# An expert layer that starts from an early tile map: 24 tiles mapped before the attention ends, 16 shared blocks in front and 16 behind

## The chip, the core and the metric

The kernel runs on one core of a Trainium2 chip. A time is the device time of one execution in microseconds (us). Three executions of the kernel before took 761.66, 758.09 and 762.01 us, with a median of 761.66 us. The core's engines run side by side, each through its own list of instructions in order: TensorE (PE in the rows, PEld for its weight loads), VectorE (DVE), ScalarE (ACT), GpSimd (POOL) and SyncE (SP), which issues most of the DMAs. They meet at semaphores.

## What is computed

Two layers, each an attention and then a mixture of 8 experts, on 32 x 128 = 4096 tokens of width 128. Only the last two parts matter here:

```python
x = x + attention_1(layernorm(x), ctx)        # 16 heads, window of 64, rotary angles
xf = layernorm(x).reshape(4096, 128)
scores = softmax(xf @ gate_w.T)
idx = top_k(scores + gate_b, 2)               # two of 8 experts for each token
rw = scores at idx, else 0
expert(x, w1, b1, w3, b3, w2, b2) = silu((x @ w1 + b1) * (x @ w3 + b3)) @ w2 + b2
y = sum over experts of rw * expert_e(xf)     # the routed part: 8192 (token, expert) pairs
z = expert_shared(xf)                         # the shared part: every token
x = x + y + z
```

## The kernel before

**The attention of layer 1** handles one block of 128 tokens in a step k of a loop to k = 32, and the last blocks in twelve named steps, `TAIL`: "divide", "turn last but one", "products last but one", "normalise last", "turn last", "products last", "softmax last", "choose last", "rank last", "fills", "tiles" and "maps". The router runs along with it, over groups of 4 or 2 blocks (`GROUPS_AT[1]`). VectorE chooses the experts of a group (`choose`, L829 to L847), TensorE counts how many tokens each expert has so far (`ranks`, L1155; the rank of the group at step k of `RANK_AT`), VectorE adds that to the running totals `carry` and writes each token's place (`place_reads` and `place`, L850 to L870). GpSimd then scatters the tokens' rows to their expert's region in DRAM, two indirect DMAs for each block (`scatter`, L533). The first four groups (16 blocks) are ranked by k = 24 and the last one in "rank last".

**The maps.** In "fills", "tiles" and "maps" VectorE turns the final totals into two tables (L1013 to L1045): `emap`, the expert of each tile, and `rowmap`, the DRAM row where the tile starts. A tile is 128 rows of one expert, and there are `SLOTS` = 71 of them. SyncE waits for the totals, fills up each expert's last tile (`fill_up`, L351), waits for the maps and for every scatter (`rows_in_place`), and only then loads tile 0.

**The expert layer** (`gated_experts`) works in units (`UNITS`). A shared unit is two blocks of the shared expert, which needs no map: first products `widen` (L1776), two copies on ScalarE (L1666, L1667), the product of the halves on VectorE (`hidden`, L1707), silu on ScalarE (L1672, L1674), second products `narrow` (L1789), and an addition to `x` on VectorE (L1722). A routed unit is two tiles. SyncE loads them into one of 16 places of `xs` (L1591), TensorE turns them (`take`, L1756), VectorE copies the expert's weights (`w1_copies`, L1697), then the same chain (L1770, L1663, L1704, L1672, L1789), and VectorE scales each result into one of 8 places of `ys` (L1716). GpSimd scatters each tile's results to DRAM by an indirect DMA (`send`, L1640), with indices that `note` (L1632) has copied from `xs` to `xi` once for each pair. VectorE may write a place of `ys` only when the scatter of eight tiles earlier has landed.

The order is 11 shared units (22 blocks, `SHARED_FIRST`), 36 routed units, 5 shared units. Each unit has two halves in every engine's list, and a half stands behind each of the twelve `TAIL` steps (`SLOTS_AT`); the rest follow. The PE halves are: first half `widen` of its own unit, second half `narrow` of the unit two before.

**The end.** SyncE waits for all scatters (`results_stored`), loads the results of all tokens in ten DMAs (L1608), VectorE adds them in eight steps of four blocks (`add_results`, L1730 and L1731), and SyncE stores `x` in five DMAs (L1614).

## Time and profile before

| | us |
|---|---|
| median of three runs | 761.66 |
| the profiled execution | 763.85 |
| its span, first to last instruction | 762.0 |
| PE busy in the span | 667.7 (88%) |
| DVE busy | 545.3 (72%) |
| POOL busy | 500.1 (66%) |
| ACT busy | 410.8 (54%) |
| mean granted TensorE clock | 0.954 of full |

In the profile, all times are from the span's start. The attention of layer 1 lies at 400 to 594 us, its twelve last steps with shared units between them at 594 to 620, more shared units to 634, the routed units to 722, five shared units to 736, and the loading, adding and storing of the end to 762. A timeline row is: start, duration, engine, line, operation, output<-input, shapes, count, and in brackets how long the engine sat idle before it and what released it.

### The profile page before, as it was taken

To read this page: it belongs to the slowest core of one execution; us is meant where nothing else is said; L and a number is where in the kernel's file an instruction comes from. 1 tells how busy PE (TensorE), PEld (TensorE's weight loads), DVE (VectorE), ACT (ScalarE), POOL (GpSimd) and SP (SyncE) were. 2 spreads that over 40 slices of the span, in tenths; PEclk is the share of its full clock that TensorE was granted. 3 is DMA by queue.
4 is the path that set the end of the run, shared out by engine and by line. 5 is a ranking of instruction groups with operands and counts; after the bars stand their busy time and mean duration, and the time that the engine had idled before them with its cause. 6 is when DMAs were issued, how large, how long until landed. Compare 5 with 4: busy or idle time off the path is not lost.

```text
span 762.0 us, 20655 instructions
## 1 busy us (share of the span) xinstructions
PE 667.7 (88%) x6884; PEld 560.4 (74%) x6884; DVE 545.3 (72%) x1634; ACT 410.8 (54%) x1054; POOL 500.1 (66%) x850
## 2 busy tenths in 40 slices
PE   6599999988798999799998999999998779999950
PEld 4477777766567989799985777777776569999950
DVE  3579999999842674244425889999998667888735
ACT  2246555555554333234415777777775657777740
POOL 5354488788764897578745553777877762888850
PEclk9799999999999999899997999999999999999985
DMA  8192000000104522322211100111001133333229
GB/s 233 45 375 52 5 27 26 27 30 31 36 33 108 158 58 75 110 72 68 72 57 53 29 17 28 44 41 54 24 27 33 36 105 83 104 103 104 76 80 288
DMA packets 60988, 57.69 MB, mean 76 GB/s; under 512 B 11347, under 2 KB 54006, under 8 KB 60342
## 3 DMA queue, kind: packets, MB, share of 16 engines
q1 hardware_dynamic: 52246, 38.41, 18.0%
q0 software_dynamic: 8640, 17.97, 6.9%
q8 instruction: 58, 0.95, 0.5%
q14 instruction: 44, 0.36, 0.2%
HBM read 33.77 MB, written 22.08 MB: 73 GB/s over the span
## 4 chain that ended last, share of the span: by engine, by line
POOL 26%; PE 26%; DVE 22%; issue 16%; DMA 4%; ACT 2%; SPq 2%; POOLq 1%; DVEq 0%
POOL results L1353 9%; PE S L1770 6%; POOL rows L533 5%; DVE mx L908 5%; DVE pr L909 5%; PE ptp L1789 4%; PE S L1095 3%; POOL xi L1346 3%; PE S L1097 3%; POOL rstd L471 2%; PE M L1128 2%; DVE stats L789 2%; DMA results<-early,xi 2%; PE ptp L1113 2%; PE ptp L1067 2%
## 5 line engine op out<-in xcount | busy, mean ns | idle before, releaser
L533 POOL DMA_INDIRECT rows<-out_rows,posi x128 | 127.5, 996 | 47.9 <-issue 28.7
L672 ACT ACTIVATE pT<-ptp 128x512 f32<-128x512 f32 (+1 forms) x192 | 94.3, 524 | 101.6 <-PE ptp L1113 90.4
L908 DVE TENSOR_REDUCE mx<-S 128x16 f32<-128x1232 f32 x64 | 91.2, 1425 | 15.1 <-PE S L1097 14.4
L1353 POOL DMA_INDIRECT results<-early,xi x71 | 75.1, 1058 | 35.7 <-DVE early L1416 29.2
L909 DVE TENSOR_TENSOR pr<-S,mx 128x1232 f32<-128x1232 f32 x64 | 92.2, 1441 | 2.2
L1640 POOL DMA_INDIRECT results<-early,xi x71 | 70.4, 991 | 25.5 <-DVE early L1716 13.2
L1442 PE MATMUL S<-early,w1s 128*128 128x128 f32 x568 | 76.5, 278 | 3.8 <-DVE w1s L1409 3.0
L1452 PE MATMUL S<-first_w,early 128*128 x568 | 76.9, 279 | 0.8 <-DVE early L1416 0.7
L1128 PE MATMUL M<-pT,vm 128*32 128x128 f32 (+1 forms) x2048 | 70.3, 278 | 6.3 <-POOL vm L495 6.3
L1416 DVE TENSOR_SCALAR early<-S,xs 128x128 f32<-128x128 f32 x71 | 24.8, 349 | 69.2 <-PE S L1452 61.4
L1442 PEld LDWEIGHTS S<-early,w1s 128*128 128x128 f32 x568 | 69.9, 194 | 5.2 <-issue 4.4
L1388 ACT ACTIVATE early<-S 128x128 f32<-128x128 f32 x71 | 19.7, 278 | 97.0 <-PE S L1435 97.0
L1452 PEld LDWEIGHTS S<-first_w,early 128*128 128x128 f32 x568 | 70.1, 194 | 1.8 <-issue 1.5
L1113 PE MATMUL ptp<-cst,pr 128*128 128x128 f32 x512 | 68.9, 279 | 0.0
L1095 PE MATMUL S<-kexp,qT 32*128 32x308 f32 x512 | 53.6, 488 | 16.0 <-DVE pr L909 9.3
L1128 PEld LDWEIGHTS M<-pT,vm 128*32 128x32 f32 (+1 forms) x2048 | 52.6, 111 | 18.4 <-issue 11.0
L1113 PEld LDWEIGHTS ptp<-cst,pr 128*128 128x128 f32 x512 | 61.9, 145 | 2.6
L469 POOL TENSOR_TENSOR negm<-zero,mv 128x4 f32<-128x4 f32 x40 | 8.1, 203 | 82.5 <-DVE mv L792 80.8
L1789 PE MATMUL ptp<-W,kT 128*128 (+1 forms) x412 | 55.5, 279 | 2.1 <-ACT kT L1674 0.9
L1789 PEld LDWEIGHTS ptp<-W,kT 128*128 128x128 f32 x412 | 51.7, 195 | 4.2 <-issue 2.2
L1770 PE MATMUL S<-early,w1s 128*128 128x128 f32 x426 | 53.4, 275 | 0.0
L1770 PEld LDWEIGHTS S<-early,w1s 128*128 128x128 f32 x426 | 50.5, 192 | 0.0
(190 smaller groups left out, 1581.4 us busy)
## 6 DMA issues: line engine op xcount, KB each, us to landing
xs<-rows SPq DMA_DIRECT2D x142, 66.0 KB, 1.8
first_w<-in_e_W SPq DMA_DIRECT2D x2, 2048.0 KB, 10.8
swap<-results SPq DMA_DIRECT2D x32, 128.0 KB
first_w<-results SPq DMA_DIRECT2D x6, 512.0 KB, 7.2
results<-early,xi POOLq DMA_INDIRECT x142, 2.4
rows<-out_rows,posi POOLq DMA_INDIRECT x128, 2.3
W1r<-in_e_W SPq DMA_DIRECT2D x1, 1536.0 KB, 15.3
out_x<-x_res SPq DMA_DIRECT2D x3, 512.0 KB, 6.4
```

Source lines behind the costliest of these rows:

```text
L533: nc.gpsimd.indirect_dma_start(rows[:, :], bass.IndirectOffsetOnAxis(posi[:, k, n:n + 1], 0), out_rows[:, ring_slot(groups, n), k, :], Non ...
L672: nc.scalar.activation(pT[0:rows_of, G * r:G * r + count, :], ptp[q % 2][0:rows_of, 0:count, :], ACT.Exp, scale=SCALE)\
L908: do(V.tensor_reduce(mx[:, :].rearrange("p (g j) -> p g j", g=G), sc, AX.X, ALU.max))
L909: V.tensor_tensor(pr[:, n % 2, :, :].rearrange("p (g j) k -> p g j k", g=G), sc, mx[:, :].rearrange("p (g j) -> p g j", g=G).unsqueeze(3). ...
L1095: nc.tensor.matmul(S[:, g, 0:GK], qT[heads, n % 2, :], kexp[heads, n % 2, :, :], start=True, stop=False)
L1113: last = nc.tensor.transpose(ptp[q % 2][:, g, :], flat[:, g // 2, at:at + 128], ident)
L1128: last = nc.tensor.matmul(OT[32 * g:32 * g + 32, half * T:(half + 1) * T], vm[0:rows_of, n % 2, block + g, :], pT[0:rows_of, chunk, :], st ...
L1353: nc.gpsimd.indirect_dma_start(results[:, :], bass.IndirectOffsetOnAxis(xi[:, s:s + 1], 0), ys[:, s, :], None)\
L1442: last = nc.tensor.matmul(hTp[n % 2][:, c, :], w1s[:, n % 2, c * 128:(c + 1) * 128], xsT[:, n % 3, :], start=True, stop=True)
L1452: last = nc.tensor.matmul(yp, hT[:, n % 2, c, :], w2[:, c, :], start=(c == 0), stop=(c == FC - 1))
L1770: last = nc.tensor.matmul(out[:, at * 128:(at + 1) * 128], w1s[:, u % 2, at, c * 128:(c + 1) * 128], xsT[:, r % 3, at, :], start=True, sto ...
L1789: last = nc.tensor.matmul(yp(u)[:, at, :], hT[:, u % 2, c * 256 + at * 128:c * 256 + (at + 1) * 128], w2[:, c, :], start=(c == 0), stop=(c ...
```

## The change

Five things change.

1. `SHARED_FIRST` goes from 22 to 16: 8 shared units stand in front of the routed ones and 8 behind.
2. `SLOTS_AT` places two halves instead of one behind the first five `TAIL` steps. With the other seven that makes 17 halves within `TAIL` instead of 12.
3. An early map of 24 tiles. After the steps k = 25, 26 and 27 VectorE runs the three parts of `early_map`, from the totals of the first four groups: only tiles already full count, and 24 of them always are. SyncE, once the scatters of these groups have landed, loads tiles 0 to 15 before the attention has ended, then fills up, then loads 16 to 23, and waits for the final maps and all scatters only ahead of tile 24. TensorE waits for the early map in front of the first routed unit and for the final one before tile 24. The final map covers the other 47 tiles.
4. `note` and `xi` go: `send` takes the indices straight from `xs`. So a place of `xs` is loaded again only when the scatter of the tile that it held has landed.
5. `add_results` may run for four of its eight steps from unit `ADDS_FROM` on, and its stores wait on a semaphore of their own. `GROUPS_AT[1]` gets other lanes (semaphores) for groups 6 to 8.

```diff
-    ...(20, 2, 4, 1), (22, 2, 6, 2), (24, 4, 8, 3), (28, 4, 12, 0)))
+    ...(20, 2, 4, 1), (22, 2, 6, 1), (24, 4, 8, 2), (28, 4, 12, 3)))
-SHARED_FIRST = 22
+SHARED_FIRST = 16
+EARLY, EARLY_GROUPS, EARLY_AT = 24, 4, 24
+ADDS_AFTER, HALVES_EARLY = 7, 4
-SLOTS_AT = {step: 1 for step in TAIL}
+SLOTS_AT = {step: 2 if step in TAIL[:5] else 1 for step in TAIL}
+ADDS_FROM = ROUTED_AT + len(range(0, SLOTS, 2)) + ADDS_AFTER
...
+        def early_map(part):
+            full, cu, eb = st["full"], st["full_u"], st["early_big"]
+            slot, by, of = cst[:, C_SLOT:C_SLOT + EARLY], *slots_of(EARLY)
+            if part == 0:
+                do(V.tensor_tensor(full[:, 0, :], carry[:, EARLY_GROUPS % 2, :], cst[:, C_FIRST:C_FIRST + E], ALU.subtract))
+                do(V.tensor_copy(cu[:, 0, :], full[:, 0, :]))
+                do(V.tensor_scalar(cu[:, 1, :], cu[:, 0, :], 7, None, ALU.logical_shift_right))
+                do(V.tensor_copy(full[:, 0, :], cu[:, 1, :]))
+                do(V.tensor_tensor_scan(full[:, 1, :], st["one"][:, :], full[:, 0, :], 0.0, ALU.mult, ALU.add))
+                steps.mark(V.tensor_scalar(full[:, 2, :], full[:, 1, :], float(EARLY), None, ALU.min))
+                do(V.tensor_scalar(full[:, 0, :], full[:, 0, :], -128.0, float(REGION), ALU.mult, ALU.add))
+            if part == 1:
+                do(V.tensor_tensor(eb[:, 0, :, 0:E - 1], by(slot), of(full[:, 1, 0:E - 1]), ALU.is_ge))
+                steps.mark(V.tensor_reduce(st["early_slot"][:, 0, :], eb[:, 0, :, 0:E - 1], AX.X, ALU.add))
+                do(V.tensor_tensor(eb[:, 1, :, 0:E - 1], eb[:, 0, :, 0:E - 1], of(full[:, 0, 0:E - 1]), ALU.mult))
+                do(V.tensor_reduce(st["early_slot"][:, 1, :], eb[:, 1, :, 0:E - 1], AX.X, ALU.add))
+            if part == 2:
+                steps.mark(V.tensor_copy(st["emap"][:, 0:EARLY], st["early_slot"][:, 0, :]))
+                do(V.scalar_tensor_tensor(st["early_slot"][:, 1, :], slot, 128.0, st["early_slot"][:, 1, :], ALU.mult, ALU.add))
+                V.tensor_copy(st["rowmap"][:, 0:EARLY], st["early_slot"][:, 1, :]).then_inc(maps_done, 1)
+                steps.mark(V.tensor_scalar(st["first128"][:, :], full[:, 2, 0:1], 128.0, None, ALU.mult))
+                steps.mark(V.tensor_tensor(full[:, 0, 0:E - 1], full[:, 2, 1:E], full[:, 2, 0:E - 1], ALU.subtract))
+                dve.wait_ge(maps_done, 1)
...
+            if rope and EARLY_AT < k <= EARLY_AT + 3:
+                dve.wait_ge(products_taken, k + 3)
+                early_map(k - EARLY_AT - 1)
...
+        count, done = (SLOTS - EARLY, EARLY) if rope else (SLOTS, 0)
+            do(V.tensor_tensor(tmap[:, 2, :], tmap[:, 2, :], full[:, 2, :], ALU.subtract))
+            do(V.scalar_tensor_tensor(tmap[:, 3, 0:E - 1], full[:, 0, 0:E - 1], 128.0, tmap[:, 3, 0:E - 1], ALU.mult, ALU.add))
+            do(V.tensor_scalar(slot_row, slot_row, st["first128"][:, 0:1], None, ALU.add))
...
     def load(sp, i, row=None):
         if i >= XU:
-            sp.wait_ge(xsT_ready, r + 1)
-            sp.wait_ge(xi_copied, r + 1)
-            sp.wait_ge(ys_ready, i - XU + 1)
+            sp.wait_ge(xsT_ready, before // 2 + 1)
+            sp.wait_ge(ys_ready, before + 1)
+            sp.wait_ge(ys_out[before % U], 16 * (before // U) + 16)
...
     def gpsimd(pool):
-        def note(r):
...
         def send(i):
-            s = i % U
+            s, place = i % U, xs[:, i % XU, IDX:IDX + 1].bitcast(U32)
+            in_place(pool, i)
             pool.wait_ge(ys_ready, i + 1)
-            pool.wait_ge(xi_copied, i // 2 + 1)
-            nc.gpsimd.indirect_dma_start(results[:, :], bass.IndirectOffsetOnAxis(xi[:, s:s + 1], 0), ys[:, s, :], None)\
-                .then_inc(ys_out[s], 16)
+            nc.gpsimd.indirect_dma_start(results[:, :], bass.IndirectOffsetOnAxis(place, 0), ys[:, s, :], None).then_inc(ys_out[s], 16)
...
+            if u - 2 >= ADDS_FROM and halves < HALVES_EARLY:
+                dve.wait_ge(z_ready, pairs_through(u - 3))
+                add_results(halves)
+                halves += 1
...
             run(a1["sync"](sp))
-            row = a1["rows_in_place"](sp, e1["first_row"])
-            e1["load"](sp, 0, row)
-            for i in range(1, SLOTS):
+            a1["early_set"](sp)
+            a1["early_rows"](sp)
+            for i in range(min(16, EARLY)):
+                e1["load"](sp, i)
+            a1["fill_up"](sp, range(E - 1, -1, -1))
+            for i in range(16, EARLY):
+                e1["load"](sp, i)
+            a1["maps_set"](sp)
+            a1["rows_landed"](sp)
+            for i in range(EARLY, SLOTS):
                 e1["load"](sp, i)
```

## Rows read from the trace of the kernel before

**Rows 1.** Windows, all engines: stretch, length, busy and count each, clock, DMA.

```profile
400.00:560.00 160.00, 150.76 (x1835) 112.82 (x1834) 139.42 (x410) 114.91 (x332) 101.88 (x205) 0.97 0.12 36
...
600.00:610.00 10.00, 7.28 (x39) 6.35 (x39) 5.60 (x28) 6.47 (x12) 7.64 (x12) 0.83 0.12 41
...
640.00:660.00 20.00, 20.00 (x182) 20.00 (x181) 16.34 (x49) 14.85 (x41) 14.37 (x19) 1.00 0.37 99
```

**Rows 2.** Timeline of POOL: last row scatter, first two pairs of result scatters, last two.

```profile
625.71 0.96 POOL L533 DMA_INDIRECT rows<-out_rows,posi  x1 [0.30 <-issue]
...
642.42 1.13 POOL L1640 DMA_INDIRECT results<-early,xi  x1 [9.15 <-DVE early L1716]
643.86 0.96 POOL L1640 DMA_INDIRECT results<-early,xi  x1 [0.31 <-issue]
644.85 0.20 POOL L1632 TENSOR_TENSOR xi<-xs,zero 128x2 uint32<-128x2 uint32 x1
645.21 1.14 POOL L1640 DMA_INDIRECT results<-early,xi  x1 [0.16 <-issue]
...
735.06 0.96 POOL L1640 DMA_INDIRECT results<-early,xi  x1 [0.31 <-issue]
736.33 0.96 POOL L1640 DMA_INDIRECT results<-early,xi  x1 [0.30 <-issue]
```

**Rows 3.** Timeline of SP, 704 to 762: issues merged.

```profile
738.72 11.64 SPq L1608 DMA_DIRECT2D first_w<-results  x10
```

**Rows 4.** DMA issues, 600 to 762: last number is median us to landing.

```profile
xs<-rows SPq DMA_DIRECT2D x71, 66.0 KB, 1.8
...
results<-early,xi POOLq DMA_INDIRECT x71, 2.3
```

**Rows 5.** Timeline of PE: two neighbouring routed units; first shared unit behind.

```profile
705.58 1.50 PE L1770 MATMUL S<-early,w1s 128*128 128x128 f32 x12
...
708.03 1.50 PE L1770 MATMUL S<-early,w1s 128*128 128x128 f32 x12
...
722.03 1.46 PE L1776 MATMUL S<-xall,W1s 128*128 128x256 f32 x6
```

**Rows 6.** Timelines of DVE and POOL in the attention's last steps of the loop.

```profile
548.28 1.44 DVE L908 TENSOR_REDUCE mx<-S 128x16 f32<-128x1232 f32 x1 [0.36 <-PE S L1097]
...
574.78 0.17 DVE L870 CAST posi<-posf 128x8 uint32<-128x8 f32 x1
...
575.23 1.01 POOL L533 DMA_INDIRECT rows<-out_rows,posi  x1 [1.30 <-DVE posi L870]
```

**Rows 7.** Timeline of DVE: operations of the maps.

```profile
618.75 0.17 DVE L1019 TENSOR_SCALAR tiles_u<-tiles 128x8 uint32<-128x8 f32 x1
618.95 0.17 DVE L1020 TENSOR_SCALAR tiles_u<-tiles_u 128x8 uint32<-128x8 uint32 x1
...
620.11 0.68 DVE L1036 TENSOR_TENSOR pT<-cst,tiles 128x497 f32<-128x497 f32 x1
```

**Rows 8.** Timeline of PE in the attention's end, to the first routed unit.

```profile
603.46 2.46 PE L1776 MATMUL S<-xall,W1s 128*128 128x256 f32 x6
...
607.76 1.46 PE L1776 MATMUL S<-xall,W1s 128*128 128x256 f32 x6
...
613.83 0.18 PE L1158 MATMUL M<-both,beforeb 128*128 128x32 bf16 x1 [3.72 <-DVE both L842]
...
634.53 1.50 PE L1770 MATMUL S<-early,w1s 128*128 128x128 f32 x12
```

**Rows 9.** Timeline of ACT: the first copies of two shared units behind the attention.

```profile
626.00 0.47 ACT L1666 ACTIVATE pr<-S,bsh 128x256 f32<-128x256 f32 x1
...
627.95 0.47 ACT L1666 ACTIVATE pr<-S,bsh 128x256 f32<-128x256 f32 x1
```

**Rows 10.** Timeline of DVE: last addition of a shared unit, second step of the final additions.

```profile
735.54 0.42 DVE L1722 TENSOR_TENSOR x_res<-x_res,ptp 128x256 f32<-128x256 f32 x1 [1.11 <-PE ptp L1789]
...
745.16 0.69 DVE L1730 TENSOR_TENSOR x_res<-x_res,first_w 128x512 f32<-128x512 f32 x1 [0.98 <-DMA first_w<-results]
```

More of the change, by code:

```diff
@@ L421, in rows_in_place, with rows_landed @@
         maps_set(sp)
-        row = first_row(sp)
+        row = first_row(sp) if first_row else None
+        rows_landed(sp)
+        return row
+    def rows_landed(sp):
         rows_scattered(sp)
         sp.wait_ge(filled, 16 * E)
-        return row
     def first_loads(sp):
@@ L1257, in maps_set, with early_set, early_rows @@
     def maps_set(eng):
+        eng.wait_ge(maps_done, 2 if rope else 1)
+    def early_set(eng):
         eng.wait_ge(maps_done, 1)
+    def early_rows(sp):
+        for g in range(EARLY_GROUPS):
+            sp.wait_ge(scattered[lane(groups, g)], 32 * in_lane(groups, g))
     def x_updated(dve, n):
@@ L1623, in gpsimd @@
     def gpsimd(pool):
-        def note(r):
-            own = range(2 * r, min(2 * r + 2, SLOTS))
-            for i in own:
-                wait(pool, ys_out[i % U], 16 * (i // U))
-                in_place(pool, i)
-            s, xat, size = own[0] % U, own[0] % XU, len(own)
-            nc.gpsimd.tensor_tensor(xi[:, s:s + size], xs[:, xat:xat + size, IDX].bitcast(U32), st["zero"][:, 0:size], ALU.add)\
-                .then_inc(xi_copied, 1)
         def send(i):
-            s = i % U
+            s, place = i % U, xs[:, i % XU, IDX:IDX + 1].bitcast(U32)
+            in_place(pool, i)
             pool.wait_ge(ys_ready, i + 1)
-            pool.wait_ge(xi_copied, i // 2 + 1)
-            nc.gpsimd.indirect_dma_start(results[:, :], bass.IndirectOffsetOnAxis(xi[:, s:s + 1], 0), ys[:, s, :], None)\
-                .then_inc(ys_out[s], 16)
-        note(0)
+            nc.gpsimd.indirect_dma_start(results[:, :], bass.IndirectOffsetOnAxis(place, 0), ys[:, s, :], None).then_inc(ys_out[s], 16)
         for i in range(SLOTS):
-            if i % 2 == 0 and i + 2 < SLOTS:
-                note(i // 2 + 1)
             send(i)
@@ L1741, in vector @@
                 results_of(u - 2)
+            if u - 2 >= ADDS_FROM and halves < HALVES_EARLY:
+                dve.wait_ge(z_ready, pairs_through(u - 3))
+                add_results(halves)
+                halves += 1
             yield u
         dve.wait_ge(z_ready, pairs_through(NU - 1))
-        for half in range(B // HU):
+        for half in range(halves, B // HU):
             add_results(half)
@@ L1804, in tensor @@
                 narrow(u - 1, None)
-                maps_set(pe)
+                early_set(pe)
                 for v in (ROUTED_AT, ROUTED_AT + 1):
```

55 lines of the change are left out of this document (33 added, 22 removed), and 2 rows, old and new, of the table GROUPS_AT.

## The prediction, made before the changed kernel had run

> **What bounds the kernel now.** I read four views in this order. The windows show where TensorE is not full: it is busy 20.00 of 20 us in the routed stretch, but 7.28 of 10 at a granted clock of 0.83 in the attention's end [rows 1]. That end is a gap that more shared work could fill. Next the tail of the span. SyncE starts to load the results at 738.72 [rows 3], right after the last scatter, and TensorE's part is over sooner: the last addition of a shared unit ends at 735.54 + 0.42 = 735.96 [rows 10]. So not TensorE but the last result scatter sets the end. GpSimd issues it at 736.33 [rows 2], and from there to the end of the span is 762.0 - 736.33 = 25.7 us of landing, loads, additions and stores. Third, what sets 736.33: 71 scatters from 642.42 on, 93.91 us for 70 intervals, 1.342 us each [rows 2]. TensorE needs 708.03 - 705.58 = 2.45 us for a unit of two tiles [rows 5], 1.23 a tile. GpSimd is the slower of the two, since a pair also has its copy of indices (643.86 to 645.21 is 1.35, of which 0.20 is the copy). Fourth, what sets 642.42: the first routed products at 634.53 [rows 8], with 7.9 us between, while GpSimd had been free since 626.67 and idle for 9.15 at the last [rows 2]. So the time is: start of the first routed unit + 7.9 + 70 scatter intervals + 25.7.
>
> **The change part by part.**
>
> *The early map* is new work on VectorE in steps k = 25, 26, 27. Part 0 has 7 operations on 8 columns. Such operations start 618.95 - 618.75 = 0.20 apart [rows 7], so 1.4. Part 1 has 4 operations on 24 x 7 = 168 columns. By the rows 8 columns take 0.20 from start to start and 497 take 0.68 + 0.03; between them 168 give 0.20 + 160/489 x 0.51 = 0.37, so 1.5. Part 2 has 5 small ones, 0.9 with its wait. Sum 3.8, less 0.1 where two follow without a wait: 3.7 us. Is it covered? VectorE is busy 139.42 of 160 us before [rows 1], but in this stretch its only idle time over 0.1 us that I found from 547 to 574 is the 0.36 at 548.28, ahead of the first part, and GpSimd then waits 1.30 for VectorE's places at 575.23 [rows 6]. Bounds: 1.5 us (if the slack of the neighbours takes more than half) and 4.5 (if each of the three new waits drains the engine). I take all 3.7, as VectorE has no idle row there.
>
> *Two halves instead of one behind five steps.* The last rank needs VectorE's `choose last`. Before, four `hidden` (units 0 to 3) stand ahead of it in VectorE's list; after, six (0 to 5), and a seventh ahead of `place` and the fills. A `hidden` waits for TensorE's products and ScalarE's copies, so each adds not its own 0.9 but the round of a shared unit, 627.95 - 626.00 = 1.95 us [rows 9]. Three of them make 5.9 us. Bounds: nothing (if the new halves only fill waits such as the 3.72 of TensorE at 613.83 [rows 8]) and 10 us (if all five extra halves cost a round). I take 5.8, since the waits that they would fill are on TensorE and this chain runs through VectorE and ScalarE. The last rank then starts at 613.83 + 3.7 + 5.8 = 623.3.
>
> *The first routed unit* no longer waits for the final maps, the fills and the loads. Before, 634.53 - 613.83 = 20.7 us lie between last rank and first routed products, filled with seven `widen` of shared units. After, only one is left (unit 7), with four `narrow` and the first turns; on VectorE the places, the fills, the weight copy, `hidden` and two thirds of the maps. Two rounds of 1.95 and some 3.8 us of VectorE's small operations give 7.7. First routed products: 623.3 + 7.7 = 631.0, which is 3.5 us earlier than before; bounds 628 and 636. GpSimd's eight last row scatters also move, by 3.7 + 5.8, to an end at 626.67 + 9.5 = 636.2. The first result scatter at 631.0 + 7.9 = 638.9 comes 2.7 us later, so they are just covered; past that slack each us costs one.
>
> *Loads of tiles 0 to 15* move into the attention, where DMA engines are busy 0.12 of the time [rows 1], and cost nothing. The fills move behind them on SyncE, and tile 16 behind the fills and the first scatter: 638.9 + 2.3 landing + 1.8 load [rows 4] = 643.0. TensorE turns it two units ahead of unit 16, at 631.0 + 6 x 2.45 = 645.7 at the earliest. It is in time.
>
> *No copy of indices.* GpSimd's two sends with nothing between start 736.33 - 735.06 = 1.27 apart [rows 2]; I take 1.28 for every tile, against 1.342. 70 x 0.062 = 4.3 us. Bounds: 1.25 to 1.34. TensorE still feeds it: last routed products at 631.0 + 35 x 2.45 = 716.8, plus 7.9 = 724.7, before the last send at 638.9 + 70 x 1.28 = 728.5.
>
> *The final map* has 47 x 7 = 329 columns instead of 497 in four operations, 4 x 168/489 x 0.51 = 0.7 less, and three more small ones, 0.6 more: nothing. The other lanes give nothing. Of the four additions allowed ahead, only one can run, as `ADDS_FROM` is 51 and the last unit of the loop is 53: nothing. The heading of the change speaks of 10 tiles in front; the diff has 16 blocks, and the diff is what I cost.
>
> *Eight shared units behind instead of five.* Routed products take 722.03 - 634.53 = 87.5, so they end at 718.5. Five units took 735.96 - 722.03 = 13.9, some 2.8 each with stalls, 1.95 without [rows 9]; three more at 2.4 make 7.1: the last addition ends at 739.5. The loads start at 738.72 - 7.8 = 730.9. The first store can be issued only when SyncE has issued ten loads, 11.64 us later [rows 3], and needs the second addition step, 1.4 us long: 739.5 + 1.4 = 740.9 against 742.5. So the eight units are hidden with 1.6 us to spare.
>
> **The sum.** First send 3.5 us earlier, 70 intervals 4.3 us shorter, the 25.7 us behind unchanged: 7.8 us. The span would be 754.2 and the profiled execution 763.85 - 7.8 = 756.1. That execution lay 2.2 above the median, so for the median 761.66 - 7.8 = 753.9.
>
> **The rivals.**
>
> *The attention's end stretches more than I counted.* The last rank or GpSimd's row scatters come 3.5 us later than above (the upper bound of the halves, 10 us, does it), and the first send is no earlier than 642.4. Only the 4.3 us of the intervals are left: 757.4. For it: every step there waits for another engine. Chance 17%.
>
> *The shared units behind become the end.* If the routed units stall or each of the eight takes 2.8 us, the last addition ends 3.4 us later or more, beyond the 1.6: 755.7 to 757. Chance 10%.
>
> *TensorE's clock.* The first products of a shared unit took 2.46 us at 603.46 and 1.46 at 607.76 [rows 8], and the stretch had a granted clock of 0.83 [rows 1], between the levels of 1.2 and 2.4 GHz, after TensorE had waited. With twice the halves it waits less. If the clock stays up, some two such units are 1.0 us shorter each on the path to the last rank, and the clock holds to the first routed unit: 2 to 2.5 us more gain, 751.5. Chance 10%. The Trainium skill (TensorE: Matmul & The Clock Gate, Part 1) says that the default state is throttled and that activity releases the throttle; by it this rival is the rule, while the 3.72 us wait of [rows 8], which the change doesn't remove, speaks for 753.9.
>
> *Slower: the ring through `xs` becomes the pace.* A load now waits for the landing of the scatter 16 tiles earlier, and SyncE's loads are in order. Round the ring: landing 2.3, issue 0.4, load 1.8 [rows 4], then turn, two units of lead (4.9) and 7.9 to the result, 17.3 us, and 16 tiles at 1.28 allow 20.5. It decides the pace above 20.5, eats the gain at 16 x 1.39 = 22.3, and at 24 us (for example a landing that takes 4 us and a load that takes 4 at the DMA share of 0.37 [rows 1], with two us of GpSimd's queue) the interval is 1.50: 70 x 0.22 = 15.4 more, 769.3. Chance 6%. The Trainium skill (DMA: Bandwidth & Descriptors, Anatomy of one DMA) gives about 2.0 us as fixed cost whatever the size; by it the new wait costs that much once per turn of the ring and stays within the slack of 3.2, and the 2.3 and 1.8 of [rows 4] agree.
>
> *No change:* the later start cancels the shorter intervals, or the sends are no closer than before (1.34, with the indices read from `xs`) and the start gains little: 760 to 762. Chance 7%.
>
> **How the numbers follow.** Forecast 50%, the others 17, 10, 10, 6 and 7. The predicted time is 753.9. Its own bounds, from 628 to 636 for the first routed products, give 751 to 758; with the clock and a pace of 1.25 on the one side, the stretched end and half of the no-change case on the other, the range is 748.5 to 759.5. A measurement of this kernel can tell about 0.5%, 3.8 us, so faster means under 757.9. Forecast, clock and units behind, and half of the stretched end lie there: 0.79. Within it 0.14, slower 0.07.
>
> **What would show it.** In the profile after: the loads of `xs` at about 580 us; VectorE's early map as 16 operations of 3.7 us in total and the last rank near 623; the first routed products near 631 and first send near 639; sends 1.28 apart without `xi`; the last send near 728.5 and SyncE's result loads near 731; the last shared addition near 739.5. The prediction is wrong if the sends start after 642, if TensorE waits for `xs` in the routed stretch, or if the final additions wait for a shared unit rather than for a DMA.

## The result: 755.65 us, 0.6% faster

Seven executions of the changed kernel took 754.67 to 758.61 us with a median of 755.65; seven of the kernel before took 758.09 to 762.57 with a median of 761.66. The ratio is 0.9935, with a 95% interval of 0.9918 to 0.9951. The profiled execution took 757.13 us and its span is 755.3. In a second series (label `after_2`, below) the ratio was 0.9944. Ratios leave out the executions in which the chip was in its slower state (such as two of the ten of b_noxi, at 780.52 and 1267.85 us), and can differ by up to 0.2% from the quotient of the medians given.

The lines of the changed kernel have moved: the row scatter is L539, the loads of `xs` L1646, `send` L1685, the result loads L1663, the stores L1669, `take` L1802, routed and shared first products L1816 and L1822, second products L1835, the weight copies L1738, the addition of a shared unit L1763, the final additions L1771 and L1772.

First the windows, in the columns of [rows 1] (stretch, length, busy and count of PE, PEld, DVE, ACT, POOL, clock, DMA share, GB/s):

```profile
600.00:610.00 10.00, 9.69 (x59) 8.91 (x59) 7.31 (x38) 7.27 (x18) 6.69 (x11) 0.83 0.10 35
610.00:620.00 10.00, 6.62 (x40) 5.66 (x41) 7.67 (x41) 7.21 (x14) 6.62 (x9) 0.93 0.15 49
620.00:630.00 10.00, 6.81 (x43) 6.10 (x42) 8.45 (x28) 4.40 (x11) 7.39 (x8) 0.84 0.56 150
640.00:660.00 20.00, 19.29 (x171) 18.83 (x170) 16.04 (x47) 14.23 (x39) 14.83 (x16) 1.00 0.37 104
```

The doubled halves fill TensorE at 600 to 610, 9.69 us instead of the 7.28 of [rows 1], at the same granted clock of 0.83. In the routed stretch it is the other way round: TensorE was full and now stands still 0.71 of 20 us.

Then the early map on VectorE, part 1 and the steps around it (timeline of DVE; `mx` is the first operation of each step of the attention's loop):

```profile
553.65 1.41 DVE L914 TENSOR_REDUCE mx<-S 128x16 f32<-128x1232 f32 x1
...
558.05 0.33 DVE L953 TENSOR_TENSOR early_big<-cst,full 128x168 f32<-128x168 f32 x1
558.42 0.33 DVE L954 TENSOR_REDUCE early_slot<-early_big 128x24 f32<-128x168 f32 x1
558.67 0.53 DVE L955 TENSOR_TENSOR early_big<-early_big,full 128x168 f32<-128x168 f32 x1
559.23 0.33 DVE L956 TENSOR_REDUCE early_slot<-early_big 128x24 f32<-128x168 f32 x1
...
560.10 1.43 DVE L914 TENSOR_REDUCE mx<-S 128x16 f32<-128x1232 f32 x1
```

The step takes 560.10 - 553.65 = 6.45 us with four new operations in it, and no idle time stands in brackets anywhere. Then the last rank and the first routed units (timeline of PE):

```profile
617.27 0.18 PE L1203 MATMUL M<-both,beforeb 128*128 128x32 bf16 x1 [3.36 <-DVE both L848]
...
624.48 1.50 PE L1816 MATMUL S<-early,w1s 128*128 128x128 f32 x12
...
628.84 2.90 PE L1816 MATMUL S<-early,w1s 128*128 128x128 f32 x12 [2.64 <-DVE w1s L1738]
```

The first routed products start 10 us earlier than in [rows 8], but the second unit waits 2.64 us for its weight copy. VectorE makes that copy only after the final map, which has no cover of shared units any more (timeline of DVE):

```profile
627.14 0.26 DVE L1090 CAST rowmap<-slot_f 128x47 int32<-128x47 f32 x1
627.87 0.82 DVE L1738 COPY w1s<-W1r 128x384 f32 x2 [0.48 <-DVE rowmap L1090]
```

GpSimd's last row scatter, its first sends and its last one (timeline of POOL, to be laid beside [rows 2]):

```profile
628.43 1.09 POOL L539 DMA_INDIRECT rows<-out_rows,posi  x1 [0.30 <-issue]
636.76 0.96 POOL L1685 DMA_INDIRECT results<-early,xs  x1 [7.23 <-DVE early L1757]
638.02 0.96 POOL L1685 DMA_INDIRECT results<-early,xs  x1 [0.30 <-issue]
...
728.33 0.96 POOL L1685 DMA_INDIRECT results<-early,xs  x1 [0.30 <-issue]
```

The first send is 5.66 us earlier than before, and neighbours are 1.26 apart. All 70 intervals take 728.33 - 636.76 = 91.57, 1.308 each.

Last, the loads of tiles 0 to 15 and the end (timelines of SP and DVE):

```profile
575.10 13.99 SPq L1646 DMA_DIRECT2D xs<-rows  x16
...
731.16 12.47 SPq L1663 DMA_DIRECT2D first_w<-results  x10
743.67 8.53 SPq L1669 DMA_DIRECT2D out_x<-x_res  x5
```
```profile
739.50 0.42 DVE L1763 TENSOR_TENSOR x_res<-x_res,ptp 128x256 f32<-128x256 f32 x1 [0.97 <-PE ptp L1835]
739.84 0.68 DVE L1771 TENSOR_TENSOR x_res<-x_res,first_w 128x512 f32<-128x512 f32 x1
...
749.05 0.69 DVE L1771 TENSOR_TENSOR x_res<-x_res,first_w 128x512 f32<-128x512 f32 x1 [0.74 <-DMA first_w<-results]
...
751.10 0.69 DVE L1772 TENSOR_TENSOR x_res<-x_res,first_w 128x512 f32<-128x512 f32 x1
```

From the last send to the span's end it is 755.3 - 728.33 = 26.97 us instead of 25.67. So the span moves by -5.66 (start of the sends), -2.34 (their intervals) and +1.30 (the end), together -6.7 us.

The start can be cut further, from row to row of both kernels (shift of after against before):

| event | before | after | shift | change of shift |
|---|---|---|---|---|
| `mx` of the step ahead of the early map | 548.28 | 545.78 | -2.50 | -2.5 |
| last `mx` | 585.16 | 586.44 | +1.28 | +3.8 |
| last rank | 613.83 | 617.27 | +3.44 | +2.2 |
| first routed products | 634.53 | 624.48 | -10.05 | -13.5 |
| first send | 642.42 | 636.76 | -5.66 | +4.4 |

The first -2.5 lies ahead of the early map and of everything behind it, so I put it down to the two profiled executions. The row lies at 545.9 to 549.3 in the four profiles without the map and at 544.6 to 548.2 in the six with it on chips of this speed, so single profiles differ by as much. The profile of before lay 2.2 us above its median, that of after 1.5 above its own.

### The profile page after: what moved, and what is told of

Read it like the earlier page. It is cut to its first block, busy times and chain, and to the rows that moved or that the text cites. A ratio compares the mean times of both kernels' runs of the same rounds, so it can differ in the third digit from the quotient of the medians.

```text
span 755.3 us, 20579 instructions
## 1 busy us (share of the span) xinstructions
PE 669.2 (89%) x6884; PEld 560.6 (74%) x6884; DVE 548.6 (73%) x1653; ACT 410.3 (54%) x1054; POOL 490.7 (65%) x814
## 4 chain that ended last, share of the span: by engine, by line
PE 28%; DVE 25%; POOL 23%; issue 15%; DMA 3%; ACT 2%; SPq 2%; POOLq 0%; DVEq 0%; ACTq 0%
POOL results L1408 9%; PE S L1816 6%; DVE mx L914 6%; DVE pr L915 5%; PE ptp L1835 5%; POOL rows L539 4%; PE S L1140 3%; POOL xi L1401 3%; PE S L1142 3%; DVE stats L795 2%; PE M L1173 2%; POOL rstd L477 2%; PE ptp L1158 2%; SPq L1663 1%; PE ptp L1112 1%
## 5 line engine op out<-in xcount | busy, mean ns | idle before, releaser
L539 POOL DMA_INDIRECT rows<-out_rows,posi x128 | 127.2, 994 | 50.0 <-issue 29.1
L1408 POOL DMA_INDIRECT results<-early,xi x71 | 75.3, 1061 | 36.6 <-DVE early L1471 30.0
L1685 POOL DMA_INDIRECT results<-early,xs x71 | 69.6, 980 | 30.2 <-issue 19.1
L1497 PE MATMUL S<-early,w1s 128*128 128x128 f32 x568 | 78.0, 282 | 3.8 <-DVE w1s L1464 3.0
L1497 PEld LDWEIGHTS S<-early,w1s 128*128 128x128 f32 x568 | 71.5, 198 | 5.3 <-issue 4.4
L1835 PE MATMUL ptp<-W,kT 128*128 (+1 forms) x412 | 56.4, 282 | 2.8 <-issue 2.3
L1816 PE MATMUL S<-early,w1s 128*128 128x128 f32 x426 | 54.9, 280 | 2.6 <-DVE w1s L1738 2.6
L1835 PEld LDWEIGHTS ptp<-W,kT 128*128 128x128 f32 x412 | 52.5, 196 | 6.0 <-issue 4.5
L1816 PEld LDWEIGHTS S<-early,w1s 128*128 128x128 f32 x426 | 51.7, 196 | 2.8 <-issue 2.8
```

The lines of the kernel that those rows point to most:

```text
L539: nc.gpsimd.indirect_dma_start(rows[:, :], bass.IndirectOffsetOnAxis(posi[:, k, n:n + 1], 0), out_rows[:, ring_slot(groups, n), k, :], Non ...
L1408: nc.gpsimd.indirect_dma_start(results[:, :], bass.IndirectOffsetOnAxis(xi[:, s:s + 1], 0), ys[:, s, :], None)\
L1497: last = nc.tensor.matmul(hTp[n % 2][:, c, :], w1s[:, n % 2, c * 128:(c + 1) * 128], xsT[:, n % 3, :], start=True, stop=True)
L1816: last = nc.tensor.matmul(out[:, at * 128:(at + 1) * 128], w1s[:, u % 2, at, c * 128:(c + 1) * 128], xsT[:, r % 3, at, :], start=True, sto ...
L1835: last = nc.tensor.matmul(yp(u)[:, at, :], hT[:, u % 2, c * 256 + at * 128:c * 256 + (at + 1) * 128], w2[:, c, :], start=(c == 0), stop=(c ...
```

## The experiments

Ratios are to the kernel before on the same chip, with the 95% interval.

### One part of the change alone, in the kernel before

**b_front16**: 16 shared blocks in front instead of 22, nothing else.

```diff
-SHARED_FIRST = 22
+SHARED_FIRST = 16
```

> The kernel before with one edit: 16 shared blocks in front of the routed units and 16 behind, instead of 22 and 10. No early map. My theory (start of the routed units + 71 sends + end): the routed units can't start before SyncE's loads, which began at 628.7 and gave their first tiles at 631.4 in the kernel before, so they start at about 631.9 instead of 634.5, and the sends keep their 1.34 us: 2.6 us less than before, some 759.1. Rival (fewer shared units in front are the whole gain, the early map adds nothing): 6 us less, 755.7. Both expect the same times as before up to the attention's end; if the last steps of layer 1 again lie 2.4 us off the kernel before, that shift is no part of the change.

Measured: 761.57 us, ratio 1.0005 (0.9987 to 1.0022). Both expected times failed. The first send came at 641.4, one us earlier than before, and the last at 736.15. But the attention's last `mx` was 2.0 us earlier in this execution (583.12 instead of 585.16); counted from there the first send was 1.0 us later (58.3 us instead of 57.3). TensorE ran out of shared work and waited for tiles (timeline of PE of b_front16):

```profile
629.58 0.47 PE L1756 MATMUL M<-cst,xs 128*128 128x128 f32 x1 [3.90 <-DMA xs<-rows]
```

So moving shared units behind brings nothing while the first tile can't be loaded sooner.

**b_noxi**: the kernel before without the copies of indices, so that a load of `xs` waits for the landed scatter of 16 tiles earlier.

```diff
-            sp.wait_ge(xsT_ready, r + 1)
-            sp.wait_ge(xi_copied, r + 1)
-            sp.wait_ge(ys_ready, i - XU + 1)
+            sp.wait_ge(xsT_ready, before // 2 + 1)
+            sp.wait_ge(ys_ready, before + 1)
+            sp.wait_ge(ys_out[before % U], 16 * (before // U) + 16)
...
-            pool.wait_ge(xi_copied, i // 2 + 1)
-            ...IndirectOffsetOnAxis(xi[:, s:s + 1], 0)...
+            ...IndirectOffsetOnAxis(place, 0)...
```

> The kernel before with one edit: no copy of indices, the sends take them from xs, and a load waits for the landing of the scatter 16 tiles earlier. My theory (GpSimd's interval paces the sends): interval 1.28 instead of 1.34, 4.3 us less, 757.4. Rival (the trace of the changed kernel shows 1.31 and short waits of TensorE that nothing in the profile releases, so TensorE paces without the copies): 2.3 us less, 759.4. Third, the ring through xs costs what the copies did: no change.

Measured: 761.49 us, ratio 0.9997 (0.9976 to 1.0017). The median interval was 1.26, but the mean 1.326, and in the windows of b_noxi TensorE is no longer full:

```profile
680.00:700.00 20.00, 18.60 (x160) 17.88 (x160) 14.92 (x44) 13.40 (x37) 14.26 (x15) 1.00 0.37 105
```

What the copies cost, the new wait of the loads takes back. That was the third expectation.

**b_f16_noxi**: both edits together. It is the changed kernel without the early map, with one half behind each step and without part 5 of the change (the additions ahead and the lanes).

> The kernel before with 16 shared blocks in front (22 behind stay as the other 16) and without the copies of indices, the loads waiting for landed scatters as in the changed kernel. It is the changed kernel with one half per step and without the early map, so against a_slots1 (756.9) it tells what the early map is worth. Neither edit alone changed the time. Theory (the early map carries the gain, because only it lets the routed units start before the last maps): first send as in b_front16, 641.4, intervals as in b_noxi, 1.326, last send 734.2, the end 25.7 to 27: a span of 760 to 761, no change within 0.3%. Rival (the two parts need each other: with fewer units in front the ring through xs runs freely, 1.28 per send): 641.4 + 70 x 1.28 = 731.0, a span of 757, ratio 0.995, and the early map would then be worth next to nothing.

Measured: 762.45 us, ratio 1.0000 (0.9979 to 1.0022). The theory's verdict held: the parts don't gain together what they don't gain alone. Its first send did not, 645.2 instead of 641.4: GpSimd waits long for its first result (timeline of POOL of b_f16_noxi):

```profile
645.22 1.07 POOL L1630 DMA_INDIRECT results<-early,xs  x1 [17.46 <-DVE early L1702]
...
738.16 0.96 POOL L1630 DMA_INDIRECT results<-early,xs  x1 [0.30 <-issue]
```

### One part of the change undone

**a_slots1**: the changed kernel with one half behind each step.

```diff
-SLOTS_AT = {step: 2 if step in TAIL[:5] else 1 for step in TAIL}
+SLOTS_AT = {step: 1 for step in TAIL}
```

> The changed kernel with one half unit behind each of the twelve last steps, as before, instead of two behind the first five. My theory as the prediction had it: the last rank 5.8 us earlier, but 2.5 units of 2.2 us more behind it, so the first routed products at nearly the same time, time within 1 us of the changed kernel. Rival (the trace of the changed kernel: the last rank came only 2.2 us later by the extra halves): last rank 2.2 us earlier, 5.5 us of shared work behind it, first routed products 3.3 us later and the time 3 us more, 758.9.

Measured: 756.91 us, ratio 0.9962 (0.9945 to 0.9978). Against b_f16_noxi (on another chip), which lacks the early map, the early loads and part 5, that is 0.4%, and the two intervals just don't meet. None of the additions of part 5 ran ahead of the last shared one in after (739.84 behind 739.50). So the early map with its loads carries most of the gain. Against the change as a whole (0.9935 and 0.9944) the second halves are worth 0.2 to 0.3%, and there the intervals overlap. That the time would stay within 1 us came true, but not for the expected reason, a last rank 5.8 us earlier. The timelines of PE and POOL of a_slots1:

```profile
614.21 0.18 PE L1203 MATMUL M<-both,beforeb 128*128 128x32 bf16 x1 [4.36 <-DVE both L848]
...
629.29 1.50 PE L1816 MATMUL S<-early,w1s 128*128 128x128 f32 x12
...
637.67 1.08 POOL L1685 DMA_INDIRECT results<-early,xs  x1 [10.54 <-DVE early L1757]
```

The attention ended two us earlier in this execution, so the times are to be counted from its last `mx`, at 584.44 (586.44 in after, 586.72 in after_2). From there the first routed products come after 44.9 us (38.0 and 38.3), and the first send after 53.2 (50.3 and 49.0): the second halves bring the first unit 6.5 to 6.8 us forward, but the first send only 2.9 to 4.2. From the last `mx` to the last rank it is 28.7 to 29.8 us in the five profiles with single halves, and 30.8 to 31.1 in after, after_2, a_xi and a_xu24_2: 1 to 2.4 us for the halves.

**a_xi**: the changed kernel with the copies of indices and with the old waits of the loads (the diff of b_noxi, reversed).

> The changed kernel with the copies of indices and the old waits of the loads put back. My theory: sends 1.34 apart again, 2.3 to 4.3 us more than the changed kernel, 758 to 760. Rival (TensorE's own waits set 1.31 and the copies fit beside them): under 1 us more. If TensorE's short waits in the routed stretch vanish here, they belong to the new waits of the loads or to the shorter interval.

Measured: 757.1 us, ratio 0.9953 (0.9934 to 0.9973), not to be told from the change; the 758 to 760 of my theory failed. Sends are 1.336 apart again, as it said, but TensorE is full (windows of a_xi):

```profile
680.00:700.00 20.00, 20.00 (x181) 19.98 (x180) 16.70 (x49) 14.76 (x41) 16.37 (x24) 1.00 0.37 106
```

So its stops come with the new wait of the loads, and part 4 of the change is about even on balance.

### The changed kernel again, a larger ring, fewer units in front

**after_2**: the changed kernel as the neighbour of the others.

> The changed kernel itself, as the neighbour of the others on the same chip. All theories: ratio 0.9935, span near 755, first send near 636.8, last near 728.3, about ten long turns of TensorE in the routed stretch.

Measured: 756.58 us, ratio 0.9944 (0.9924 to 0.9964), first send 635.75, last 726.57 (mean interval 1.297), span 753.8.

**a_xu24_2**: 24 places of `xs` instead of 16; eight of them lie in `raw`, a buffer of the attention. A load then waits for a scatter 24 tiles back.

```diff
-    XU = 16
+    XU = 24
...
+    more = sh["raw"][:, :, :, :].rearrange("p c b d -> p (c b d)")
+    def tile_at(i, c0, c1):
+        s = i % XU
+        return xs[:, s, c0:c1] if s < 16 else more[:, (s - 16) * RW + c0:(s - 16) * RW + c1]
...
-        sp.dma_start(xs[:, s, :], rows[bass.ds(at, 128), :]).then_inc(xs_in[s], 16)
+        sp.dma_start(tile_at(i, 0, RW), rows[bass.ds(at, 128), :]).then_inc(xs_in[s], 16)
```

> The changed kernel with 24 places of xs instead of 16 (eight lie in a buffer that the attention has done with), so a load waits for a scatter 24 tiles back. The experiment a_xu24 on another chip. Theory (the ring through 16 places holds some loads back until TensorE stops): the ten turns of 2.63 to 3.27 us go, TensorE takes 2.45 per unit, sends come 1.26 apart, the last send at 636.8 + 88.2 = 725.0 instead of 728.3, and the trailing shared units end 3 to 5 us sooner, so the end is 25.7 again: a span of 751, median near 751.5, ratio 0.987. Rival (the stops have another cause, such as the order of loads on SyncE): stops and intervals of 1.31 stay, span 755, ratio 0.9935.

Measured: 754.11 us, ratio 0.9895 (0.9876 to 0.9914). That is 2.5 us below after_2, and the intervals of the two don't meet (four executions against seven): the best of all kernels here. The windows of a_xu24_2, its first send and its last:

```profile
640.00:660.00 20.00, 20.00 (x182) 20.00 (x181) 16.61 (x50) 15.12 (x42) 15.12 (x17) 1.00 0.34 101
...
680.00:700.00 20.00, 20.00 (x182) 20.00 (x181) 16.95 (x50) 15.15 (x42) 15.36 (x16) 1.00 0.39 112
```
```profile
639.25 0.96 POOL L1693 DMA_INDIRECT results<-early,xs  x1 [7.01 <-DVE early L1765]
...
728.55 0.95 POOL L1693 DMA_INDIRECT results<-early,raw  x1 [0.31 <-issue]
```

The 70 intervals take 89.3 us, 1.276 each, against 1.297 in after_2 and 1.308 in the profile of after, and from the first send on no turn comes more than 2.46 us after the one before. The expected 751.5 was too good by 2.6: a 1.26 for all intervals was assumed, and the end was 754.8 - 728.55 = 26.25 instead of 25.7. Of the 3.5 us by which its first send is later than that of after_2, 2.4 go back to the attention's last `mx` in this execution.

**a_front10_2**: 10 shared blocks in front and 22 behind, as the heading that the prediction speaks of has it.

```diff
-SHARED_FIRST = 16
+SHARED_FIRST = 10
```

> The changed kernel with 10 shared blocks in front and 22 behind, as the heading of the change says. The experiment a_front10 on another chip. Theory (the start of the sends is set by GpSimd's last row scatters and by the chain to the last rank, not by the shared units in front): first routed products 3 rounds earlier, but VectorE and TensorE then work on routed units ahead of the last rank, whose chain waits 2 to 5 us longer; three more shared units behind end 7 us later, at 746, and the additions wait for them: span 757 to 760, ratio 0.996 to 1.0. Rival (earlier routed units give earlier sends): first send at 634, last at 725.7, span 754 or less.

Measured: 757.22 us, ratio 0.9942 (0.9921 to 0.9963), no difference to after_2 at 756.58. Neither expectation came true as a whole (timelines of POOL and DVE of a_front10_2):

```profile
630.98 1.09 POOL L539 DMA_INDIRECT rows<-out_rows,posi  x1 [0.30 <-issue]
632.37 1.41 POOL L1685 DMA_INDIRECT results<-early,xs  x1 [0.30 <-DVE early L1757]
...
724.84 0.95 POOL L1685 DMA_INDIRECT results<-early,xs  x1 [0.30 <-issue]
```
```profile
744.67 0.41 DVE L1763 TENSOR_TENSOR x_res<-x_res,ptp 128x256 f32<-128x256 f32 x1
...
751.03 0.69 DVE L1772 TENSOR_TENSOR x_res<-x_res,first_w 128x512 f32<-128x512 f32 x1
```

The first send is 3.4 us earlier than in after_2 and follows right behind the last row scatter, which is now the floor. The rival had that, and nearly its times (634, 725.7 and a span of 754 or less; measured 632.4, 724.8 and 754.5). But the last send is only 1.7 earlier (mean interval 1.321), and shared units end at 744.67 + 0.41, so 754.5 - 724.84 = 29.7 us follow the last send, 2.4 more than in after_2. The last rank came 32.1 us after the last `mx`, 1.0 later than in after_2, not the expected 2 to 5. The theory had the later end (746), but not the span of 757 to 760.

### Four kernels on a chip that took 815 us

On this chip the kernel before had a median of 815.27 us (809 to 821), 7% above the other chips, and every kernel on it the like. The sum was made for the others; nothing below tells the theories apart but for one price.

**a_xu24** is the kernel of a_xu24_2, **a_front10** that of a_front10_2.

> The changed kernel with 24 places for loaded tiles instead of 16 (the eight more lie in a buffer that the attention has done with). So a load waits for the scatter 24 tiles earlier. Theory (in the changed kernel the ring send, landing, load, turn, result, send takes 14.8 us from turn to send and 2.8 + 1.9 from send to landed load, 19.5 us or more of the 20.2 that 16 tiles at 1.26 us allow, so that each load that SyncE issues 1.3 us late stops TensorE): no turn more than 2.6 us after the one before in the steady stretch instead of ten, sends 1.265 apart instead of 1.308, last send 3 us earlier, last shared addition 4 us earlier, time 3.5 to 4.3 us less than the changed kernel, about 752. Rival (the stops are TensorE's own, fetching its instructions or reading the maps): the ten stops stay and so does the time, 755.7.

> The changed kernel with 10 shared blocks in front and 22 behind, as the heading of the change has it. Theory: the first routed results are ready before GpSimd has ended its row scatters at 629.5, so the first send comes at about 631 instead of 636.8; the last send then at 722.5 instead of 728.3; but TensorE's total work is the same, so the last shared addition stays at 739.5 and the end hangs on it: four additions are done ahead, four are left, 5.6 us, and the last stores. Time 1 to 3 us less than the changed kernel, 753 to 754.5. Rival (the last send alone sets the end): 5.8 us less, 750. Rival on the other side: the sends at 631 or earlier meet the full eight places of results and hold up VectorE, and with it the last rank: no gain or slower, 756 to 760.

Measured: 815.67 us, ratio 1.0012 (0.9977 to 1.0046), and 816.2 us, ratio 1.0014 (0.9978 to 1.0049).

**a_tiles3**: three halves behind the step "tiles" instead of one, to hide the final map.

```diff
-SLOTS_AT = {step: 2 if step in TAIL[:5] else 1 for step in TAIL}
+SLOTS_AT = {step: 2 if step in TAIL[:5] else 3 if step == "tiles" else 1 for step in TAIL}
```

> The changed kernel with three halves behind the step tiles instead of one, so that VectorE copies the second routed unit's weights and does the first one's hidden part before the last part of the final map and not after it (in the changed kernel TensorE waited 2.64 us there at 628.8). Theory: the wait goes, the first send 2 us earlier at 634.8, all sends and the last addition with it: 1.5 to 2 us less, 754. Rival (the pace of the ring and TensorE's total work set the end, the first send doesn't): under 0.5 us.

Measured: 817.68 us, ratio 1.0035 (0.9997 to 1.0072). Its timeline of PE ahead of the first routed products, and its windows in the routed stretch, show what was different here:

```profile
648.67 0.69 PE L1802 MATMUL M<-cst,xs 128*128 128x128 f32 x2 [6.66 <-issue]
```
```profile
680.00:700.00 20.00, 17.01 (x131) 16.33 (x132) 10.76 (x33) 9.57 (x27) 11.48 (x12) 0.91 0.25 71
```

TensorE stands still for 6.66 us with nothing in the profile that released it. In the routed stretch TensorE runs 131 matmuls in 20 us at a granted clock of 0.91, where in after it runs 169 at 1.00, and the sends are 1.80 us apart in the mean (median 1.27). Beside that the 6 us of this change vanish. Whether three halves at "tiles" help is open.

**a_map2**: parts 0 and 1 of the early map are run twice.

```diff
                 early_map(k - EARLY_AT - 1)
+                if k < EARLY_AT + 3:
+                    early_map(k - EARLY_AT - 1)
```

> The changed kernel with parts 0 and 1 of the early map run twice in their steps (the values are the same). They took 1.4 and 1.5 us. Theory (VectorE has no slack at k = 25 and 26, so each us of the early map moves the attention's end by one): the last steps of the attention and the time 2.9 us later, 758.5. Rival (the chain through GpSimd has slack of 0.8 us or more there, as VectorE waits for TensorE at later steps): 1 to 2 us later. Second rival: nothing, since the end hangs on TensorE's total work.

Measured: 818.43 us, ratio 1.0042 (1.0003 to 1.0081). The time says little, the profile more: VectorE's steps are regular here too. The step with part 0 takes 574.72 - 565.50 = 9.22 us instead of the 553.65 - 545.78 = 7.87 of after (timeline of DVE of a_map2):

```profile
565.50 1.44 DVE L914 TENSOR_REDUCE mx<-S 128x16 f32<-128x1232 f32 x1 [0.36 <-PE S L1144]
574.72 1.41 DVE L914 TENSOR_REDUCE mx<-S 128x16 f32<-128x1232 f32 x1
```

That is 1.35 more, and the next step 7.96 instead of 6.45, 1.51 more. Doubled, the map's operations cost their full length once more.

## Why the prediction was right, and which of its steps were not

The forecast of 753.9 us is 1.75 us below the 755.65, and 2.7 below the 756.58 of after_2. The likeliest case was the one that came: the last send sets the end, it comes earlier by an earlier first unit and by closer sends. But the sizes of its terms were off, and two errors of 4 us cancelled. Of its three signs of being wrong, one came (TensorE stops in the routed stretch for late tiles of `xs`) and one came in part: the first four steps of the final additions ran behind the last shared addition, the rest waited for DMAs. Its steps:

**Early map: 3.7 predicted, 3.7 measured.** With the map the three steps take 7.87, 6.45 and 7.68 us, 22.0 in all; without it 6.17, 5.00 and 7.13, 18.3 (before, from 548.28 [rows 6] on). Each of the six profiles with the map on the other chips has 21.9 to 22.1. Choosing no cover was right: VectorE had no idle row there. The length of part 1 was well read from two widths [rows 7]: 168 columns took 0.33 to 0.53 us an operation.

**Two halves: 5.8 predicted, 1 to 2.4 measured.** This is the term that was mis-sized. I priced each added `hidden` by a round of 1.95 us [rows 9], on the ground that the waits to be filled were TensorE's alone. They were not: TensorE's wait for the last choice only fell from 3.72 [rows 8] to 3.36, but from 600 to 610 TensorE went from 7.28 to 9.69 busy, VectorE from 5.60 to 7.31 and ScalarE from 6.47 to 7.27. A round measured behind the attention, where nothing else waits, is no price for a round inside a chain with holes. The last rank came at 617.3 instead of 623.3, of which 2.5 are the shift of the profiles.

**Last rank to first routed products: 7.7 predicted, 7.2 measured.** They came at 624.5 instead of 631.0, for the reason just given.

**First products to first send: 7.9 taken over, 12.3 measured.** This step failed and cancelled the one before. The 7.9 of [rows 2, 8] hold when three units follow each other. Here the second unit's weight copy stands behind the final map in VectorE's list, and TensorE waits 2.64 us for it; later units come behind. Then the second unit's twelve products took 2.90 us instead of the 1.50 of the first: the granted clock was 0.59 from 628 to 632, so the lower level had come in behind that wait. In after_2, with the same wait, it was 1.00 there (timeline of PE of after_2):

```profile
629.42 1.57 PE L1816 MATMUL S<-early,w1s 128*128 128x128 f32 x12 [2.65 <-DVE w1s L1738]
```

So in after_2 the way to the first send was 10.7, in a_slots1, where the first products start at 629.29 and the map is sooner done with, 8.4. So of the 6.5 to 6.8 us that the second halves gain for the first unit, 2.9 to 4.2 reach the first send. The first send at 638.9 was thus nearly right, 636.8, or 639.3 with the shift of the profiles taken out. GpSimd's row scatters, predicted to end at 636.2, ended at 629.5 and were no limit.

**Intervals: 1.28 predicted, 1.308 and 1.297 measured.** Two neighbours are 1.26 apart, so the price of a send was right. What is missing is the ring, my slower rival, in a mild form. I reckoned 17.3 us round it. The rows around 650 us (POOL, SP and PE of after) show one that didn't fit:

```profile
648.28 0.95 POOL L1685 DMA_INDIRECT results<-early,xs  x1 [0.30 <-issue]
...
652.39 0.33 SPq L1646 DMA_DIRECT2D xs<-rows  x1
```
```profile
651.46 0.38 PE L1802 MATMUL M<-cst,xs 128*128 128x128 f32 x2
652.11 1.15 PE L1835 MATMUL ptp<-W,kT 128*128 x8 [0.27 <-issue]
653.10 1.50 PE L1816 MATMUL S<-early,w1s 128*128 128x128 f32 x12
654.44 0.38 PE L1802 MATMUL M<-cst,xs 128*128 128x128 f32 x2
655.26 1.15 PE L1835 MATMUL ptp<-W,kT 128*128 x8 [0.44 <-issue]
```

The load behind the scatter of 648.28 is issued 4.1 us later; with the 1.9 us to its landing it arrives at 654.2, 0.3 us ahead of its turn (the second of the two at 654.44). The turn itself doesn't wait, but in TensorE's list two reads of the experts of the pair (L1628) stand between the wait for its tiles and the next second products. They begin at 654.27 and take 0.31 and 0.36 us, so the second products start 0.82 us after the turn, not 0.22 as elsewhere, and the next turn comes at 657.59, 3.15 after the one of 654.44 instead of 2.45. The 2.98 before it is the same with the load issued at 647.41, which landed after 3.3 us. Most loads are issued 2.8 us after their scatter, as reckoned (2.7). But every four or five units one pair has 3.7 to 4.8, five pairs in after, and these land with only 0.2 to 0.5 us to spare for their second tile; all nine long turns behind the start of the stretch, 2.63 to 3.27 us, stand at them or right behind them. The way from turn to send is 14.2 to 15.4 us for a second tile, not 4.9 + 7.9 = 12.8. Part of it is GpSimd's queue: in a_xu24_2 it grows from 14.5 to 16.8, since GpSimd needs 1.26 a tile and TensorE 1.23. Round the ring that makes 2.8 + 1.9 + 14.7 = 19.4, and 16 tiles at 1.26 allow 20.2: 0.8 us of slack, of which the two reads take most, and any late load eats it. b_noxi has the stops without the rest of the change, a_xi has the change without the stops, and a_xu24_2 has the new wait but no stops, with the ring larger. So the cause is shown: the new wait on a ring of 16.

Why some transfers come late can be read from the same trace. The scatter of 647.02 landed after 3.9 us and that of 648.28 after 3.1, where most take 2.2 to 2.5. The trace has 16 signals for each landing; of the scatter of 647.02 fifteen had come by 649.39 and the last came at 650.95. In that time one packet of 16 KB, 1.42 us long, moved on another queue, from 648.07 on (DMA queues of after, 647 to 649.6, then 636 to 706: packets, MB, share):

```profile
q8 instruction: 1, 0.02, 3.4%
...
q8 instruction: 5, 0.08, 0.6%
```

These five packets (648.07, 659.19, 672.14, 685.06, 698.68) begin 1.0 to 1.6 us after the first scatter of each of the five late pairs, and no other of that size moved in the stretch. The five late pairs of after_2 and the six of b_noxi have one each as well. a_xu24_2 has the packets and the late loads too (up to 4.6 us after the scatter), but they land with 8 us or more to spare. No run took the packets away, so this rests on their coincidence.

**The end: 0 predicted, +1.3 measured.** The last shared addition started at 739.50, where its end was predicted, and the final additions then ran on to a wait for a DMA at 749.05, not for a shared unit. So my rival of the shared units behind did not decide it. The 1.3 consist of 0.44 more from the last send to the first result load (2.83 instead of 2.39) and 0.85 more from there to the last addition (19.94 instead of 19.09 between 738.72 [rows 3] and 757.81). The 0.44 is again a late landing: a packet of `q8 instruction` began at 728.83, and the last scatter landed after 2.7 us instead of 2.2. The four of the ten profiles in which such a packet began within a us of the last send (after, after_2, a_slots1, a_front10_2) have 2.8 to 3.3 us to the first result load, the other six 2.4. Of the 0.85 I know only that the loads were issued in 12.5 us, not in 11.6. The number of shared units doesn't explain it: in b_f16_noxi they ended at 749.9, all eight steps of the additions ran behind them without a wait, and the end was still 25.6; in a_xu24_2 they ended at 737.6 and it was 26.25. With three more of them in the changed kernel (a_front10_2) the last steps run behind them, and the end was 29.7.

**TensorE's clock.** The rival of a clock that stays up did not come: 0.83 at 600 to 610 as before, although TensorE was busy 9.69 of 10 us, then 0.93 and 0.84. In after_2, with equal code, 590 to 640 had 0.96 instead of 0.90, and 600 to 610 had 1.00. But its last rank came 31.1 us after the last `mx`, not sooner than the 30.8 of after, so the higher level bought nothing on that path. By the rule of the Trainium skill (TensorE: Matmul & The Clock Gate, Part 1), that activity releases the throttle, the fuller stretch should have gained; the window of 600 to 610 shows that in after_2 (1.00, TensorE busy 8.20 of 10 us), and not in after (0.83, busy 9.69) or in a_xi (0.83, busy 10.00).

**The sum.** Predicted: -3.5, -4.3 and 0, together -7.8. Measured: -5.7, -2.3 and +1.3, together -6.7, of which some 2.5 at the start are the shift of the profiles. Without that shift the profiles give -4.2, and the medians give -6.0 and -5.1; the 1.8 between -4.2 and -6.0 no row places, and the profile of after_2, with a span of 753.8, is 8.2 below before. The sum came out close by luck: the halves that cost about 4 us too much in it and the second unit's wait and lower clock that it lacked (4.4) cancel each other. In the profile the ring (2.0 us beyond 1.28 a send) and the end (1.3), less the 2.1 by which the first send was early, give the 1.1 us by which the span of 755.3 is above the forecast 754.2.

## What to carry to other kernels

Removing a copy (here, of indices) that let a buffer go free early lengthens the ring through that buffer by the way to its last reader and that reader's landing; add up the whole way from rows, the queue of the last engine too, and want more slack than one late transfer takes. A gap ahead of a late stage is closed by what lets its first load start, not by moving filler work: fewer units in front and no copies of indices were worth nothing, alone or together; with the early map it was 0.4%, with the second halves too 0.6%, and with a ring of 24 it was 1.0%. Price operations added to an engine without idle rows at their full length, and added to a chain with holes well below a full round.

## What the runs showed of the hardware

GpSimd's indirect scatters of a tile run 1.26 us from start to start (0.96 busy, 0.30 with nothing that released it), whether the indices lie in a tile of 128 x 2 or inside a row buffer. A load that follows a scatter's landing was issued 2.8 us after the start of the scatter mostly, but 3.7 to 4.8 in one of four or five units; in each of these 16 cases (after, after_2, b_noxi) one 16 KB packet of the queue that the profile calls `q8 instruction` was moving, 0.9 to 1.6 us long, and of a scatter's 16 landing signals the last came up to 2.0 us behind the others (the scatter of 683.69 in after). Twelve routed products took 2.90 us at a granted clock of 0.59 and 1.57 at 1.00, in two executions of equal code, both behind a wait of TensorE of 2.64 us. And chips differ more than kernels do here: one ran the kernel before in 815.27 us instead of 761, with a stop of TensorE of 6.66 us that the profile puts down to nothing and a granted clock of 0.91 in the routed stretch, so a gain of 0.6% could not be measured on it.
